# A two-layer graph attention kernel: edge blocks that layer 1 reads back from DRAM, or makes anew from the adjacency matrix

## The reference, cut to what matters

```python
h = jnp.maximum(_layernorm(x), 0.0)          # x: (8192, 128)
x = x + _L0_gnn_ref(h, L0_gnn_W, L0_gnn_a, adj, 8192)
h = jnp.maximum(_layernorm(x), 0.0)
x = x + _L1_gnn_ref(h, adj, L1_gnn_W, L1_gnn_a)

# either layer, in short (adj: (8192, 8192) int32, the same for both):
Wh = h @ W
e = leaky_relu((Wh @ a[:128])[:, None] + (Wh @ a[128:])[None, :], 0.2)
attention = softmax(where(adj > 0, e, very_low), axis=1)
# layer 0 also drops attention under 1e-4, multiplies by the row's number of edges,
# and returns elu(Wh + attention @ Wh); layer 1 returns attention @ Wh
```

## Time and profile before

| | |
|---|---|
| median of 3 runs | 2171.67 us (2162.83 to 2172.93) |
| the profiled execution | 2169.75 us |
| its span | 2167.9 us |
| busy: TensorE, VectorE, ScalarE, GpSimd | 90%, 75%, 38%, 29% of the span |
| mean granted TensorE clock | 0.956 of 2.4 GHz |
| read from DRAM, written to DRAM | 365.04 MB, 79.82 MB |

### The profile page before, as it was taken

One profiled execution on the slowest core, in us unless ns is written; L12 is line 12 of the kernel. 1 busy time (PEld: TensorE's weight loads), 2 busy tenths in 40 slices (PEclk: granted clock), 3 DMA queues, 4 the chain that ended last, 5 costly groups with the idle time before them and its releaser, 6 DMA issues. The chain is left out here.

```text
span 2167.9 us, 38155 instructions
## 1 busy us (share of the span) xinstructions
PE 1944.8 (90%) x16852; PEld 1931.1 (89%) x16852; DVE 1622.1 (75%) x1877; ACT 830.0 (38%) x1212; POOL 630.1 (29%) x523
## 2 busy tenths in 40 slices
PE   0569999999898999999892699999999999999997
PEld 0468989999898999999892699999999999999997
DVE  4558877888787788878774677777777777777775
ACT  2957787877778777777601300000000000000000
POOL 3436566666666656665400000000000000000000
PEclk9789999999999999999996799999999999999998
DMA  7889999999999999999713422222232122222210
GB/s 195 272 338 362 357 317 346 344 372 352 338 353 322 340 340 365 342 356 357 271 35 90 159 106 79 98 78 79 78 98 78 65 92 79 98 77 80 79 59 12
DMA packets 156146, 447.47 MB, mean 206 GB/s; under 512 B 13504, under 2 KB 71232, under 8 KB 139328
## 3 DMA queue, kind: packets, MB, share of 16 engines
q0 software_dynamic: 73728, 268.47, 35.5%
q1 hardware_dynamic: 82240, 176.44, 23.0%
HBM read 365.04 MB, written 79.82 MB: 205 GB/s over the span
## 5 line engine op out<-in xcount | busy, mean ns | idle before, releaser
L910 PE MATMUL psum<-h_all,arena 128*128 128x129 f32 x16384 | 1867.9, 278 | 84.2 <-DVE arena L903 84.1
L910 PEld LDWEIGHTS psum<-h_all,arena 128*128 128x128 f32 x16384 | 1861.7, 194 | 89.2 <-DVE arena L903 62.9
L903 DVE SCALAR_TENSOR_TENSOR arena<-arena,rho_col 128x1024 f32<-128x1024 f32 x1024 | 1294.6, 1280 | 323.4 <-PE psum L910 313.1
L206 ACT ACTIVATE arena<-arena,half_step 128x1024 uint8<-128x1024 int32 x512 | 727.0, 1442 | 231.1 <-DMA arena<-in_adj_dram,piece_rows 227.5
L197 POOL DMA_INDIRECT arena<-in_adj_dram,piece_rows x512 | 621.0, 1213 | 430.6 <-ACT arena L206 362.0
L219 DVE STREAM_TRANSPOSE arena<-arena 128x1024 f32<-128x1024 f32 x128 | 157.8, 1236 | 115.8 <-ACT arena L206 115.8
L206 ACT ACTIVATION_READ_ACCUMULATOR arena<-arena,half_step 128x1 f32 x512 | 90.8, 177 | 0.0
L517 PE MATMUL psum<-ident,arena 128*128 128x128 f32 x128 | 27.1, 351 | 54.2 <-DVE arena L399 54.2
L517 PEld LDWEIGHTS psum<-ident,arena 128*128 128x128 f32 x128 | 21.1, 186 | 55.5 <-DVE arena L399 54.8
L525 PE MATMUL psum<-arena 128*128 128x131 f32 x256 | 46.5, 339 | 24.2 <-ACT arena L494 24.2
L525 PEld LDWEIGHTS psum<-arena 128*128 128x128 f32 x256 | 41.2, 242 | 29.4 <-ACT arena L494 29.2
(11 more groups left out here) (99 smaller groups left out, 166.7 us busy)
## 6 DMA issues: line engine op xcount, KB each, us to landing
edgesT<-arena SPq DMA_DIRECT2D x64, 1024.0 KB, 9.8
arena<-edgesT SPq DMA_DIRECT2D x64, 1024.0 KB, 4.8
arena<-in_adj_dram,piece_rows POOLq DMA_INDIRECT x512, 7.8
arena<-r_mid SPq DMA_DIRECT2D x2, 3072.0 KB, 22.5
arena<-in_x_dram SPq DMA_DIRECT2D x16, 256.0 KB, 9.1
h_mid<-h_all SPq DMA_DIRECT2D x16, 256.0 KB, 5.8
arena<-h_mid SPq DMA_DIRECT2D x8, 512.0 KB, 25.2
arena<-in_x_dram SPq DMA_DIRECT2D x32, 128.0 KB, 15.7
```

The source lines that it names most:

```text
L206: nc.scalar.activation(pack_bytes[h][:, k, a], adj_in[n % NA], ACT.Sigmoid, bias=half_step[:, 0:1], scale=STEEP, accum_out=cnt[g % 2][:, a ...
L903: return nc.vector.scalar_tensor_tensor(wT.rearrange("p (k n) -> p k n", k=BK), r_of(g), rho_col[:, j:j + 1], edge_bytes[:, (g * NSUB + j ...
L910: last = nc.tensor.matmul(acc_tile(g, k), wT[:, k * P:(k + 1) * P], h_all[:, j, :], start=(j == 0 and k % 2 == 0), stop=(j == T - 1), skip ...
```

## The change

Chunks 0 and 1 (blocks 0 to 7) are stored to DRAM and read back as before. The other 56 blocks are neither stored nor read. In layer 1 POOL gathers the pieces of chunks 2 to 15 again (448 gathers), ScalarE masks them again, without `accum_out`, and VectorE turns them again (112 turns), after the same tiles of a chunk as in layer 0. A list `PASSES` of 30 entries says which chunk is made by which pass: 16 passes in layer 0, 14 in layer 1; semaphores `masked` and `turned` count on through both layers.

```diff
@@
+KEPT = [0, 1]
+PASSES = list(range(NG * COLS)) + [c for c in range(NG * COLS) if c not in KEPT]
@@
         def piece(n):
-            g, r = n // (COLS * PIECES), n % (COLS * PIECES)
-            c, r = r // PIECES, r % PIECES
+            g, c = divmod(PASSES[n // PIECES], COLS)
+            r = n % PIECES
@@ mask_piece
+            counted = cnt[g % 2][:, a, 2 * k + h, c:c + 1] if n < NG * COLS * PIECES else None
             nc.scalar.activation(pack_bytes[h][:, k, a], adj_in[n % NA],
                                  ACT.Sigmoid, bias=half_step[:, 0:1], scale=STEEP,
-                                 accum_out=cnt[g % 2][:, a, 2 * k + h, c:c + 1]).then_inc(masked, 1)
+                                 accum_out=counted).then_inc(masked, 1)
@@
-        def turn_edges(dve, chunk, h, s):
-            block = chunk * SUBS + s
+        def stores_into(slot, below):
+            return len([b for b in range(slot, below, ER) if b // SUBS in KEPT])
+
+        def turn_edges(dve, turn, h, s):
+            block = PASSES[turn] * SUBS + s
             if s == 0:
-                dve.wait_ge(masked, chunk * PIECES + (h + 1) * BK * BK)
-            if block >= ER and h == 0:
-                dve.wait_ge(edges_stored[block % ER], 16 * (block // ER))
+                dve.wait_ge(masked, turn * PIECES + (h + 1) * BK * BK)
+            if turn < NG * COLS and h == 0 and stores_into(block % ER, block) > 0:
+                dve.wait_ge(edges_stored[block % ER], 16 * stores_into(block % ER, block))
@@ fast_path_0, sync_rows
-                        if i in (4, 7, 10, 13):
+                        if i in (4, 7, 10, 13) and chunk - 1 in KEPT:
                             store_block((chunk - 1) * SUBS + (i - 4) // 3)
@@ fast_path_1, sync_rows
                 def load_block(block):
+                    if block // SUBS not in KEPT:
+                        return
@@ fast_path_1, scalar_rows
-                pass
+                for n in range(NG * COLS * PIECES, len(PASSES) * PIECES):
+                    mask_piece(act, n)
@@ fast_path_1, vector_rows
+                turn_at = {15: (0, 0), 17: (0, 1), 19: (0, 2), 24: (0, 3), 25: (1, 0), 27: (1, 1), 29: (1, 2), 31: (1, 3)}
+                turn_of = {PASSES[i]: i for i in range(NG * COLS, len(PASSES))}
@@
-                            dve.wait_ge(edges_loaded[block % ER], 16 * (block // ER + 1))
+                            if block // SUBS in KEPT:
+                                dve.wait_ge(edges_loaded[block % ER], 16 * stores_into(block % ER, block + 1))
+                            else:
+                                dve.wait_ge(turned, turn_number(turn_of[block // SUBS], HALVES - 1, block % SUBS))
@@
+                        if m // CT + 1 in turn_of and j % CT in turn_at:
+                            h, s = turn_at[j % CT]
+                            dve.wait_ge(formed, ((m // CT + 1) * SUBS + s - ER + 1) * SBT)
+                            turn_edges(dve, turn_of[m // CT + 1], h, s)
@@ fast_path_1, pool_rows
-                pass
+                for n in range(NG * COLS * PIECES, len(PASSES) * PIECES):
+                    load_piece(pool, n)
```

More of the change, by code:

```diff
@@ L205, in mask_piece, with turn_number @@
                 act.wait_ge(turned, turn_number(n // PIECES - 1, h, SUBS - 1))
+            counted = cnt[g % 2][:, a, 2 * k + h, c:c + 1] if n < NG * COLS * PIECES else None
             nc.scalar.activation(pack_bytes[h][:, k, a], adj_in[n % NA],
                                  ACT.Sigmoid, bias=half_step[:, 0:1], scale=STEEP,
-                                 accum_out=cnt[g % 2][:, a, 2 * k + h, c:c + 1]).then_inc(masked, 1)
-        def turn_number(chunk, h, s):
-            return chunk * HALVES * SUBS + h * SUBS + s + 1
-        def turn_edges(dve, chunk, h, s):
-            block = chunk * SUBS + s
+                                 accum_out=counted).then_inc(masked, 1)
+        def turn_number(turn, h, s):
+            return turn * HALVES * SUBS + h * SUBS + s + 1
+        def stores_into(slot, below):
+            return len([b for b in range(slot, below, ER) if b // SUBS in KEPT])
+        def turn_edges(dve, turn, h, s):
+            block = PASSES[turn] * SUBS + s
             if s == 0:
-                dve.wait_ge(masked, chunk * PIECES + (h + 1) * BK * BK)
-            if block >= ER and h == 0:
-                dve.wait_ge(edges_stored[block % ER], 16 * (block // ER))
+                dve.wait_ge(masked, turn * PIECES + (h + 1) * BK * BK)
+            if turn < NG * COLS and h == 0 and stores_into(block % ER, block) > 0:
+                dve.wait_ge(edges_stored[block % ER], 16 * stores_into(block % ER, block))
             nc.vector.transpose(edge_words[:, block % ER, h],
@@ L979, in sync_rows @@
                 for i in range(ER):
-                    sp.wait_ge(edges_stored[i], 16 * len(range(i, NG * NSUB, ER)))
+                    sp.wait_ge(edges_stored[i], 16 * stores_into(i, NG * NSUB))
             def scalar_rows(act):
```

## The result

The changed kernel took 2092.34 us (median of 4 runs, 2092.04 to 2096.27) against 2168.53 us for the kernel before (2162.83 to 2172.93): a ratio of 0.9654, 95% interval 0.9625 to 0.9683. (A fourth run of the kernel before, 2165.38, moved its median from the 2171.67 that stood ahead of the prediction.) It is faster by 76 us. I had forecast 2107, and 2095 for the lowest case that I wrote down, so the median lies 14.7 us under the forecast and 2.7 under that case. The profiled execution took 2092.04 us, 77.7 us under that of before.

What follows compares the result with a forecast made beforehand. Layer 0 was taken as bound by DMA: stores make gathered pieces late, so TensorE breaks and its clock drops. From 2169.75 us: -72.6 stores, +7 lateness, 0 layer 1 work, +2.2 its start, forecast 2107; range 2095 to 2150.

Steps and rivals of the forecast that it cites:

- the lowest case: Whole kernel: no lateness at all and gathers at 1.50 us a piece, giving 2095 us.
- Breaks and lower clock behind tile 90: Layer 0 from 309.61 us on: dropping 56 stores wins 72.6 us, 50.0 idle time and 22.6 matmuls at the lower clock.
- Layer 1's cost: Gathers, masks and turns added in layer 1 cost 0, bounds 0 and 14 us (1 us in each of 14 chunks).
- The lateness left in layer 0: Layer 0 without the stores: VectorE's waits for masks of 0 to 3 us, charged 1 us for each of 7 groups, +7.
- a deadline of 116.4 us: Layer 0, half 1's masks: due 57.3 + 59.1 us after the opening, predicted to end at 112 to 116 us.
- the 2.7 that the ring hides: The ring of four tiles hides 2.7 us of a VectorE wait: VectorE waited 6.24 us, TensorE idled 3.54.
- The start of layer 1: First tile waits for r_mid, now beside six gathers: 8.8 us instead of 6.58, +2.2, bounds 0 and +6.6.
- I change nothing before 309.61: Layer 0's first two chunks still store their 8 blocks, so the time before 309.61 us, three breaks included, stays.
- The join of the counts: Layer 0 behind 309.61 us: 7 joins at 0.82 us each, 5.7 us of the 761.5 left for that stretch.
- The first (a dearer piece, 1.80 us): Gathers cost 1.80 us a piece, 57.6 a chunk; late in both layers, total 2148 us; chance 12%.
- The second, that the gather chain by itself sets the pace: At 1.97 us a piece layer 0 keeps its breaks, layer 1's 14 chunks take 63.0 us each, total 2252; chance 4%.
- The third: VectorE becomes the bound in layer 1, each gather holding up a tile 1.21 us: +29 us in 14 chunks, about 2510; 1%.

Runs made afterwards that it cites:

- blocks read back: The changed kernel with layer 1's gathers, masks and turns left out, 64 block loads reading the 8 stored blocks over and over: 2094.91 us.
- thin stores: The changed kernel with all 64 stores in layer 0 again, but of each of the 56 blocks only the first of 8 tiles stored: 2092.32 us.

## Why the prediction was right or wrong

**Right: what bounds the kernel and where the gain comes from.** The stores' bytes made the gathers late; put back alone they cost 74 us, cut to an eighth nothing. Breaks and lower clock behind tile 90 were put at 72.6 us, and that stretch lost 73.7 (834.14 to 760.42). The fourth break was indeed the first to go. Layer 1's cost was put at 0 and is 0.07 us in these two profiles, within the 0.7 by which that layer varies. Turns, tiles and finish fit as reckoned: a group of layer 1 still takes 114.62 us plus 0.23.

**Wrong: the sum came out 14 us too high,** 2106.4 against 2092.0 in the profiled executions. The mechanism was right, and what failed are sizes of terms, first of all the lateness that I left in layer 0. By terms:

- The lateness left in layer 0, "+7", was 0. This is half the miss. I had put the masks of half 1 at a deadline of 116.4 us after 112 to 116, so 0 to 4 us early, and then charged 1 us a group anyway. ScalarE's records show them 1.8 to 4.7 us ahead of the turn in each chunk of layer 0 from the fifth on, and 4.6 to 8.3 in layer 1 from its second on. The walk along the deadlines was right. The step that failed is the one behind it: it put the waits at 0 to 3 us, under the 2.7 that the ring hides, and yet added 1 us for each of 7 groups, without a row. The runs show no break at all behind tile 90.
- The start of layer 1, "+2.2", was -0.4: r_mid took 6.15 us in place of 6.58. The 8.8 us of the earlier trace rows that I took for the load among gathers is the middle of four loads that are not alike. The first load of each layer took 4.63 and 6.58 us; the other two, 18.32 and 11.06, were issued behind transfers of blocks. And gathers hardly meet this load. In the change the first gather is issued at 1147.39, behind r_mid (line 197 in the earlier trace rows is 199 here), and its first bytes move at 1152.69, when those of r_mid (1150.61 to 1153.03) are nearly through. The two profiles without gathers there have 6.58 us (before) and 6.41 (blocks read back), the others 6.11 to 6.98.

```profile
1147.18 6.15 DMA arena<-r_mid
```

```profile
1147.39 1.60 POOL L199 DMA_INDIRECT arena<-in_adj_dram,piece_rows  x1 [161.63 <-issue]
```

- "I change nothing before 309.61": 2.1 us less (tile 90 started at 307.5, 250.21 + 57.3), as the third break was 0.31 us in place of 3.48. No dropped store can have caused that: the first one was issued at 249.33, when the masks for that break were done (247.9). The kernel with the same layer 0 and 3.81 us of third break had none of the gain, so I count it as scatter. So may be the 1.5 us less between the layers besides r_mid, in view of 85.0 to 88.8; but the two kernels that store all blocks have the two longest times there (88.8 and 88.5), so a part may come with the stores, which isn't shown.
- The join of the counts costs 0.63 us, not 0.82: 115.25 us from group to group in layer 0 (342.25, 457.50) against the 114.62 of 1024 records. I took it from start to start, while the matmuls ahead were still running out. 1.1 us.

These are 7 + 2.6 + 2.1 + 1.5 + 1.1 = 14.3.

**The range failed at its lower end** because I built it from the cases' terms alone. No lateness at all gives 2169.75 - 72.6 + 2.2 = 2099, and 2097 with r_mid unchanged; the 2095 that I wrote lies 2 us under that without a term of its own. But executions of the kernel before ran from 2162.83 to 2172.93, and parts of the changed one vary by 3 us each; a range at this end has to take in both, some 5 us.

**The rivals.** The first (a dearer piece, 1.80 us) did not come, yet its reason was sound: with four buffers the time a piece is under way does set the pace. Six are enough, by the sum above with little to spare. The second, that the gather chain by itself sets the pace, is refuted by the thin stores. The third asked for longer tiles with gathers beside them, and they didn't come. In the changed kernel, line 909 from 260 to 1060 us and from 1180 to 2070 us has medians of 1284 ns in both layers (compare):

```profile
L909 DVE SCALAR_TENSOR_TENSOR arena<-arena,rho_col x447: 1232/1284/1345, 259.6 to 1059.0; 128x1024 f32<-128x1024 f32 x149
```

```profile
L909 DVE SCALAR_TENSOR_TENSOR arena<-arena,rho_col x497: 1234/1284/1353, 1179.2 to 2068.9; 128x1024 f32<-128x1024 f32 x166
```

## What to carry to other kernels

Budget each stretch by itself, in DMA time per step against the step's own time: here 235 MB of new gathers in a stretch whose engines were 24% taken cost nothing, while 59 MB of stores less in one at 90% gave 3.5%, so an intermediate result kept in DRAM is dear where it is written if that stretch is already bound by DMA, however cheap it is to read back. Then ask for the deadline: here the cost was zero up to a threshold, and past it what didn't fit fell due in the next step. A ring's depth belongs to the same budget: with four buffers the landing time set the pace, at a DMA share of 0.76. And before a median or a mean is used as a price, look whether the things that it mixes are alike; here that mistake stood in two terms, r_mid's 8.8 us and the stores' 11.9.

## What the runs showed of the hardware that I had not expected

**A gather's issue waits for a tile, not a tile for the issue.** GpSimd's timeline in the kernel before:

```profile
613.62 1.29 POOL L197 DMA_INDIRECT arena<-in_adj_dram,piece_rows  x1 [0.50 <-ACT arena L206]
615.22 1.48 POOL L197 DMA_INDIRECT arena<-in_adj_dram,piece_rows  x1 [0.30 <-ACT arena L206]
617.00 1.55 POOL L197 DMA_INDIRECT arena<-in_adj_dram,piece_rows  x1 [0.31 <-issue]
...
621.35 0.94 POOL L197 DMA_INDIRECT arena<-in_adj_dram,piece_rows  x1 [0.30 <-issue]
```

VectorE's timeline in the same stretch:

```profile
612.81 1.28 DVE L903 SCALAR_TENSOR_TENSOR arena<-arena,rho_col 128x1024 f32<-128x1024 f32 x1 [0.50 <-PE psum L910]
614.60 1.28 DVE L903 SCALAR_TENSOR_TENSOR arena<-arena,rho_col 128x1024 f32<-128x1024 f32 x1 [0.50 <-PE psum L910]
616.46 1.28 DVE L903 SCALAR_TENSOR_TENSOR arena<-arena,rho_col 128x1024 f32<-128x1024 f32 x1 [0.57 <-PE psum L910]
```

The tiles end at 614.09, 615.88 and 617.74, and each gather ends 0.81 or 0.82 us after the tile it met (614.91, 616.70, 618.55). With VectorE idle, from 620.11 to 626.36, an issue takes 0.94. That is the rule and not three cases: of the 405 gathers that start from 260 to 1080 us, 316 start beside a tile, and 231 of these end 0.78 to 0.85 us after it; the 42 that meet nothing of VectorE's have a median of 0.94. The Trainium skill, "SBUF — State Buffer", section "Who interferes with whom", has just such a wait between a VectorE instruction with two SBUF inputs and a GpSimd one that reads SBUF. These rows agree with it on GpSimd's side; on VectorE's the median tile shows nothing and the longest 0.07 us. (Gathers that start in the first 0.15 us of a tile mostly aren't longer: the one at 618.86, 0.04 us into a tile, took 0.94, and so did the median of all 65 of them.)

**Large transfers among the gathers moved more than gathers alone, in either direction.** Three stretches of 50 us with the engines fully taken, columns as in the earlier trace rows. Before, layer 0, stores among the gathers:

```profile
440.00:490.00 50.00, 49.01 (x438) 49.01 (x439) 45.74 (x39) 36.90 (x51) 32.51 (x26) 1.00 1.03 379
```

The change: layer 0 with gathers and residuals, and the start of layer 1 with loads of blocks and r among the gathers:

```profile
772.00:822.00 50.00, 50.00 (x450) 50.00 (x450) 43.17 (x37) 39.40 (x55) 33.84 (x28) 1.00 0.99 344
1160.00:1210.00 50.00, 50.00 (x448) 50.00 (x447) 38.52 (x32) 26.41 (x19) 20.13 (x19) 1.00 1.00 399
```

No 50 us from 260 to 1060 us of the change gave more than 346 GB/s, and the last row, with loads alone, has the highest rate. So it isn't the mix of directions. It is the price of each kind: 2.37 us of the engines per MB for the stores, 2.86 to 2.90 for the gathers. That is why the stores cost 10 us a chunk, and not the 11.9 that the hardware queue's mean of 2.83 had given; the residuals on the same queue, in packets of 512 bytes, are dearer (35.2 us for 9.44 MB, 3.7 per MB).
